# Attention stage of a decoder layer: three hardware loops written out, reciprocal sums moved to GpSimd, repeated score products dropped and four other products put into a gap of TensorE

## The reference, cut to what matters

```python
q = (x @ Wq + bq).reshape(1, B * N, H, hd)         # 2048 queries, 16 heads of 16
kv = (cond @ Wkv + bkv).reshape(1, -1, 2, H, hd)   # 2048 keys
q, k = _fq_sym(q * scale, axis=-1), _fq_sym(k, axis=-1)   # 8-bit grids
v = _fq_sym(v, axis=2)
attn = softmax(einsum('bhqd,bhkd->bhqk', q, k))
attn = _fq_unsigned(attn, axis=-1)                 # levels 0..255 of the row's largest weight
out = einsum('bhqk,bhkd->bhqd', attn, v) @ Wp + bp
```

## Time and profile before

| | |
|---|---|
| median of three runs | 2234.46 us (2227.49 to 2244.91) |
| the profiled execution, its own time | 2242.98 us |
| span of the profiled execution | 2241.2 us |
| mean granted TensorE clock over the span | 0.941 of full speed |
| busy share of the span | PE 82%, VectorE 75%, ScalarE 75%, GpSimd 24% |
| attention, first L1215 to last | 1206.3 to 2036.5 us, 830.2 us |
| attention in the 40 slices | about 22nd to 36th |

### The profile page before, as it was taken

One profiled execution on the slowest core, in us unless ns is written; L12 is line 12 of the kernel. 1 busy time (PEld: TensorE's weight loads), 2 busy tenths in 40 slices (PEclk: granted clock), 3 DMA queues, 4 the chain that ended last, 5 costly groups with the idle time before them and its releaser, 6 DMA issues. The chain is left out here.

```text
span 2241.2 us, 42040 instructions
## 1 busy us (share of the span) xinstructions
PE 1832.4 (82%) x12368; PEld 1273.1 (57%) x12514; DVE 1682.5 (75%) x2852; ACT 1673.6 (75%) x2987; POOL 527.5 (24%) x433
## 2 busy tenths in 40 slices
PE   6888999999999999999676667666676666664999
PEld 5776878777777777777453322222222222232887
DVE  5885676867777777777886888888878887886443
ACT  4667888888888888888368888888888887895211
POOL 2002555555555555555100000000000000002001
PEclk8998999999999999999899998899888998997999
DMA  4000000000000000000814998888888887896000
GB/s 133 15 5 29 0 28 0 28 0 28 0 28 0 28 0 28 0 28 0 174 26 83 167 166 156 154 164 164 160 152 160 161 163 150 161 166 145 10 10 19
DMA packets 566191, 173.18 MB, mean 77 GB/s; under 512 B 535168, under 2 KB 558592, under 8 KB 566144
## 3 DMA queue, kind: packets, MB, share of 16 engines
q1 hardware_dynamic: 566144, 172.57, 38.1%
HBM read 27.83 MB, written 2.10 MB: 13 GB/s over the span
## 5 line engine op out<-in xcount | busy, mean ns | idle before, releaser
L1278 ACT ACTIVATE levels<-s_ps,nb,qstep 128x512 int16<-128x512 f32 (+1 forms) x768 | 696.8, 915 | 118.8 <-DVE nb L1215 115.4
L1145 PE MATMUL s_ps<-kT,qT 128*128 128x512 bf16 x1451 | 492.0, 429 | 266.6 <-ACT levels L1278 253.4
L1204 DVE TENSOR_REDUCE mx<-s_ps 128x1 f32<-128x512 f32 (+1 forms) x768 | 636.6, 864 | 69.0 <-PE s_ps L1145 49.6
L603 DVE SCALAR_TENSOR_TENSOR xs<-x_ps,cw,xs 128x508 f32<-128x508 f32 (+2 forms) x393 | 291.1, 741 | 174.3 <-ACT xs L525 135.9
L1145 PEld LDWEIGHTS s_ps<-kT,qT 128*128 (+1 forms) x1532 | 117.7, 101 | 513.8 <-issue 488.5
L494 PE MATMUL o_ps<-wo,hid 128*128 x1024 | 242.9, 380 | 4.9 <-DVE acc L590 4.9
L659 POOL TENSOR_TENSOR hid<-y,sg 128x512 f32<-128x512 f32 x128 | 175.4, 1371 | 277.5 <-ACT sg L547 184.8
L1505 POOL MEMSET minus_half_o<- 128x4 f32 x1 | 0.1, 102 | 962.8 <-POOLq L1087 962.8
L494 PEld LDWEIGHTS o_ps<-wo,hid 128*128 128x128 f32 x1024 | 192.7, 189 | 39.5 <-issue 9.8
L1155 PEld LDWEIGHTS ao_ps<-vi,levels_T 128*128 128x128 f16 x4096 | 145.7, 98 | 82.7 <-issue 35.9
L525 ACT ACTIVATE xs<-x_ps,cb,cw 128x512 f32<-128x512 f32 x131 | 101.8, 777 | 116.5 <-PE x_ps L446 116.4
(11 more groups left out here) (200 smaller groups left out, 3220.5 us busy)
## 6 DMA issues: line engine op xcount, KB each, us to landing
w_raw<-winT_dram SPq DMA_DIRECT2D x18, 512.0 KB, 4.4
wo_raw<-woutT_dram SPq DMA_DIRECT2D x9, 512.0 KB, 5.7
kT<-zeros SPq DMA_DIRECT2D x4, 1024.0 KB, 19.4
qT<-zeros SPq DMA_DIRECT2D x4, 1024.0 KB, 16.0
levels_T<-levels SPq DMA_TRANSPOSE x256, 4.3
acc<-xT_dram SPq DMA_DIRECT2D x4, 512.0 KB, 6.1
w_bc<-winT_dram SPq DMA_DIRECT2D x16, 128.0 KB, 2.4
acc<-x_dram SPq DMA_DIRECT2D x1, 2048.0 KB, 11.5
```

The costliest lines, as they stand in the source:

```text
L603: dve.scalar_tensor_tensor(to, x_ps[:, :, 0:SEQ - s], cw[:, head, TAPS - 1 - s], to, ALU.mult, ALU.add).then_inc(chain if s < TAPS - 1 els ...
L1145: return pe.matmul(s_ps[:, BANKS[h % 2][chunk], :], qT[:, bass.ds(round_, 1), h % NH, :].rearrange("p b t -> p (b t)"), kT[:, h % NH, at:a ...
L1204: dve.tensor_reduce(mx[:, h % 2, at:at + 1], src, AX.XY if what == "cd" else AX.X, ALU.max).then_inc(max_done, 1)
L1278: act.activation(levels[:, s, at:at + banks * GT].rearrange("p (c k) -> p c k", c=banks), s_ps[:, bank:bank + banks, :], ACT.Exp, bias=nb[ ...
```

## The change: what it does

- The loops of all engines are written out over 256 units; `held` and the register waits go.
- `nstep` and `shift` are made once for all 16 rounds before the first unit, as three VectorE instructions on 128x256; `steps` goes.
- The partial sums are kept for two rounds only. GpSimd adds them and raises the total to the power -1 (three instructions on 128x16 for each round), after the last exponential of the round. `finish` on VectorE is left with the scaling, after a wait for GpSimd and for the value products. ScalarE waits for GpSimd before it overwrites the sums of two rounds ago.
- Chunk b is made once, not three times.
- `between` puts four matmuls of 256 columns each, of no use to the result, into the unused half of `ao_ps` at the start of each unit on TensorE, ahead of the wait for the exponential a. They are left out at unit 3 of rounds 1 to 15, while VectorE scales `ao_ps`.

```diff
-        nstep = sb("nstep", [P, NH])
-        shift = sb("shift", [P, NH])
+        nstep = sb("nstep", [P, BATCH, NH])
+        shift = sb("shift", [P, BATCH, NH])
-        sums = sb("sums", [P, BATCH, NH, 3])
+        sums = sb("sums", [P, 2, NH, 3])
...
         def _(pe):
...
-                    if exists(qt, h, 2):
-                        pe.wait_ge(b_exp, n + 1)
-                        pe.sem_inc(held, 1)
-                        for _ in range(2):
-                            score(qt, h + 2, "b")
-                        score(qt, h + 2, "b").then_inc(b_ready, 1)
...
+            def between():
+
+                for _ in range(4):
+                    pe.matmul(o_ps[:, E:2 * E], vi[:, 0, 0:P], vi[:, 1, :], start=True, stop=True)
...
+            for n in range(UNITS):
+                if n < NH or n % NH != LAG:
+                    between()
+                if n + 1 < UNITS:
+                    pe.wait_ge(a_exp, n + 1)
+                    score(n + 1, "a").then_inc(a_ready, 1)
+                if n + 2 < UNITS:
+                    pe.wait_ge(b_exp, n + 1)
+                    score(n + 2, "b").then_inc(b_ready, 1)
+                if n >= LAG:
+                    if n % NH == LAG and n >= NH:
+                        pe.wait_ge(scaled, n // NH)
+                    values(n - LAG)
+                if n + 2 < UNITS:
+                    pe.wait_ge(cd_exp, n + 1)
+                    score(n + 2, "c")
+                    score(n + 2, "d").then_inc(cd_ready, 1)
...
         def _(dve):
...
+            def finish(qt):
+
+                dve.wait_ge(tot_ready, qt + 1)
+                dve.wait_ge(pv_done, (qt + 1) * NH)
+                dve.tensor_tensor(att[:, qt, :].rearrange("p (h d) -> p h d", h=NH),
                                   o_ps[:, 0:E].rearrange("p (h d) -> p h d", h=NH),
+                                  rtot[:, qt % 2, :].unsqueeze(2).to_broadcast([P, NH, HD]), ALU.mult).then_inc(scaled, 1)
...
+            dve.tensor_scalar(nstep[:, :, :], qstep[:, :, :], -1.0, None, ALU.mult).then_inc(step_chain, 1)
+            dve.wait_ge(step_chain, 1)
+            dve.reciprocal(shift[:, :, :], nstep[:, :, :]).then_inc(step_chain, 1)
+            dve.wait_ge(step_chain, 2)
+            dve.tensor_scalar(shift[:, :, :], shift[:, :, :], LN255, None, ALU.mult).then_inc(step_chain, 1)
+            dve.wait_ge(step_chain, 3)
+            for n in range(UNITS):
+                maxima(n, "b")
+                if n % NH == LAG + 1 and n >= NH:
+                    finish(n // NH - 1)
+                maxima(n, "cd")
+                maxima(n, "a")
+                bias(n)
+            finish(BATCH - 1)
...
+            for n in range(UNITS):
+                act.wait_ge(nb_ready, n + 1)
+                if n % NH == 0 and n >= 2 * NH:
+                    act.wait_ge(tot_ready, n // NH - 1)
+                if n >= RING:
+                    act.wait_ge(turned[n % RING], n // RING * 16)
+                exps(n, "a", a_exp)
+                exps(n, "b", b_exp)
+                exps(n, "cd", cd_exp)
+
+        @block.gpsimd
+        def _(pool):
+            pool.memset(minus_one[:, :], -1.0).then_inc(chain, 1)
+            for qt in range(BATCH):
+                at = qt * 2 + 1
+                pool.wait_ge(cd_exp, (qt + 1) * NH)
+                if qt >= 2:
+                    pool.wait_ge(scaled, qt - 1)
+                pool.wait_ge(chain, at)
+                pool.tensor_tensor(part[:, :], sums[:, qt % 2, :, 0], sums[:, qt % 2, :, 1], ALU.add).then_inc(chain, 1)
+                pool.wait_ge(chain, at + 1)
+                pool.tensor_tensor(tot[:, :], part[:, :], sums[:, qt % 2, :, 2], ALU.add).then_inc(chain, 1)
+                pool.wait_ge(chain, at + 2)
+                pool.tensor_tensor(rtot[:, qt % 2, :], tot[:, :], minus_one[:, :], ALU.pow).then_inc(tot_ready, 1)
```

More of the change, by code:

```diff
@@ L1195, in _, with maxima @@
+            for n in range(UNITS - LAG, UNITS):
+                values(n)
         @block.vector
         def _(dve):
-            def maxima(n, h, what):
-                bank = BANKS[h % 2]
+            def maxima(n, what):
+                u = n % 2
+                bank = BANKS[u]
                 ready, at, src = {"b": (b_ready, 0, s_ps[:, bank["b"], :]),
@@ L1203, in maxima, with bias @@
                 dve.wait_ge(ready, n + 1)
-                dve.tensor_reduce(mx[:, h % 2, at:at + 1], src, AX.XY if what == "cd" else AX.X,
+                dve.tensor_reduce(mx[:, u, at:at + 1], src, AX.XY if what == "cd" else AX.X,
                                   ALU.max).then_inc(max_done, 1)
-            def bias(n, h):
-                u = h % 2
-                if not (isinstance(n, int) and n == 0):
+            def bias(n):
+                u = n % 2
+                qt, h = divmod(n, NH)
+                if n:
@@ L1249, in body @@
-            def body(qt):
-                for h in range(NH):
-                    n = qt * NH + h
-                    if exists(qt, h, 1):
-                        maxima(n + 1, h + 1, "b")
-                    if h == NH - 1 and exists(qt, h, 1):
-                        steps(qt + 1)
-                    if h == LAG and exists(qt, 0, -1):
-                        finish(qt, qt - 1)
-                    if exists(qt, h, 1):
-                        maxima(n + 1, h + 1, "cd")
-                        maxima(n + 1, h + 1, "a")
-                        bias(n + 1, h + 1)
@@ L1294, in _ @@
-            rounds(act, body)
+                               s_ps[:, bank:bank + banks, :], ACT.Exp, bias=nb[:, u:u + 1], scale=qstep[:, qt, h:h + 1],
+                               accum_out=sums[:, qt % 2, h, k:k + 1]).then_inc(done, 1)
+            for n in range(UNITS):
+                act.wait_ge(nb_ready, n + 1)
+                if n % NH == 0 and n >= 2 * NH:
+                    act.wait_ge(tot_ready, n // NH - 1)
+                if n >= RING:
+                    act.wait_ge(turned[n % RING], n // RING * 16)
+                exps(n, "a", a_exp)
+                exps(n, "b", b_exp)
+                exps(n, "cd", cd_exp)
```

148 lines of the change are left out of this document (33 added, 115 removed).

## The result

The changed kernel takes 2151.9 us (median of 4 runs, 2149.55 to 2154.47), the kernel before 2235.4 us in the same call (4 runs). The ratio is 0.9625, with a 95% interval of 0.9586 to 0.9665: 83.5 us are gone. The direction and the place were as forecast; the size was not.

What follows compares the result with a forecast made beforehand. Bound by a loop of latencies over two units in attention: 747.2 + 5.3 + 6.4 = 758.9 us instead of 830.2, +1.8 at the start, -0.7 at the end, so 2242.98 - 70.2 = 2172.8, said as 2173 us; range 2158 to 2210.

Steps and rivals of the forecast that it cites:

- What bounds the kernel: Attention stage: no engine is full; a loop of latencies over two units, with VectorE waiting 0.25 us for chunks c and d.
- Loops written out: Attention stage: a pair of units goes from 6.00 to 5.86 us, 747.2 us for 255 intervals between biases.
- a pair below 5.86: Attention stage: pairs shorter than forecast because c and d come earlier than thought; chance 0.04.
- Finish and the low stretches: Attention rounds: scaling left on VectorE costs 5.3 us, one stretch at half clock a round costs 6.4 us.
- The start: Before the first maximum: the block making the steps once for all rounds adds 1.8 us (0 to 3).
- The end: End of the attention stage: the three small operations of the last finish go, -0.7 us.
- The four products at full clock: TensorE's gap between chunks d and the next a: the products cost 0, covered by about 0.5 us.
- Rival 1: VectorE's bias waits for GpSimd's power, 1.0 us in each of 15 rounds, 15 us: 2188 us; chance 0.20.
- Rival 2: Attention rounds alternate between high and low clock: 2204 us in half of them (0.11), 2236 us in all (0.08).
- Rival 3: Transposing DMAs bound the attention stage, a pair takes 6.15 us: 2198 us; chance 0.08.
- Rival 4: TensorE's clock stays low in the attention stage and bounds it, 3.5 us a unit: 2309 us; chance 0.05.
- the turn with the steps: Turn of the hardware loop between rounds: its extra 1.12 us go 14 times, and that of round 0.

Runs made afterwards that it cites:

- a_undone: The changed kernel with everything put back except the hardware loop (increments, three copies of b without the four products, sums on VectorE, steps once a round): 2188.91 us.
- the fastest: The changed kernel with exponentials in the order a, cd, b, maxima cd, b, a, chunk b made three times and no four products: 2130.15 us.
- a_no_between: The changed kernel without the four products at the start of each unit, chunk b still made once: 2201.47 us.
- a_undone_between: The kernel of a_undone with chunk b made once and the four products instead of three copies of b: 2184.15 us.
- a_held: The changed kernel with the increments of semaphore held put back after the waits on both TensorE and VectorE: 2169.97 us.

## Why the prediction was right in direction and wrong in size

**What bounds the kernel.** Right: the loop of latencies over two units through c and d. It still shows its wait of 0.24 us once in a pair, and each increment put back into a link of it moves the pair and the stage. One reading was off without anything resting on it: the DMA share goes down to 0.79 in the slow round of rows 1, not only to 86%.

**Loops written out: "a pair goes from 6.00 to 5.87 us. I take 5.86."** This is the step that failed. I read the price of a written-out pair from round 0 of the kernel before. That round is free of the hardware loop, but not of the increments. They stand in all 16 rounds, since the written-out ones run the same body, and not only in the loop, as the words on the kernel before have it. The change takes them out as well, and I priced them nowhere. Each stood on the path, 0.06 us between the exponential and c, and 0.04 us for VectorE's ahead of the bias. Put back, they return the pair to 5.86 us. Without them it is 5.75: 127.5 x 5.75 = 733.1 us instead of 747.2, 14.1 of the 21.0 us by which the stage came out below the 758.9 us forecast. I had noted a pair below 5.86 as a case of 4 in 100, "because c and d come earlier than I think"; they do, and the reason was in the diff. For the loop alone 5.87 was right: that is the pair of a_undone.

**Finish and the low stretches: 5.3 + 6.4 us.** Mis-sized, 737.9 - 733.1 = 4.8 us together, 6.9 less than forecast. Finish costs 0.33 us (3.04 - 2.71) where it meets a full unit and nothing in the unit in which VectorE waits for c and d anyway: round 1 takes 45.96 us, just 8 x 5.75. The low stretches came, nine instead of sixteen, eight of them around unit 4 as forecast. One of them makes its round 46.21 us, 0.25 us longer, and exchanges the two kinds of unit, so that finish meets a full one in the next round (46.3 us). With three copies of b, where these stretches are missing, the whole stage is 0.8 us above its pairs (733.9 against 733.1); so finish by itself is nearly free, and some 4 of the 4.8 us come with the stretches. The three operations that left VectorE were 0.70 us, as taken, and putting them back costs 12.7 us, since the longer unit brings stretches at 1.2 GHz too.

**The start.** 1.8 us forecast; the timeline of VectorE shows the block as 2.44 us (1204.33 to 1206.77), where before it was 1.04, so +1.4:

```profile
1204.33 0.29 DVE L1206 TENSOR_SCALAR nstep<-qstep 128x256 f32<-128x256 f32 x1 [9.11 <-PEq L696]
1204.65 1.75 DVE L1208 RECIPROCAL shift<-nstep 128x256 f32<-128x256 f32 x1
1206.44 0.29 DVE L1210 TENSOR_SCALAR shift<-shift 128x256 f32<-128x256 f32 x1
1206.77 0.69 DVE L1184 TENSOR_REDUCE mx<-s_ps 128x1 f32<-128x512 f32 x1
```

**The end.** -0.7 forecast, +0.9 measured. The last scaling starts 9.20 us after the last bias, where in the kernel before, with the three small operations ahead of it, it was 9.03. So these 0.7 us did go, but the last product with the transposed levels starts 8.50 us after the last bias, where it was 7.70:

```profile
1955.63 0.60 PE L1136 MATMUL ao_ps<-vi,levels_T 128*128 128x16 f16 x16 [1.40 <-DMA levels_T<-levels]
1956.33 0.42 DVE L1202 TENSOR_TENSOR att<-ao_ps,rtot 128x256 f32<-128x256 f32 x1 [8.97 <-PE ao_ps L1136]
```

The rest lies in the output stage. Stage, first bias and end give -92.3 + 3.0 + 0.9 = -88.4 us, against 88.5 between the two profiled executions (2242.98 - 2154.47).

**The four products at full clock: 0.** Right: a's start above, and an undisturbed round takes 45.9 us with them and with three copies of b alike. That they and the single b are needed was not claimed, and the runs show that b's three copies would have done slightly better (by 5.6 us of the medians).

**Rival 1, the bias waits for the power.** Fell. The power is 2.91 us and done 3.6 us after the last exponential, where 2.90 and 3.7 were forecast, and a bias stands inside it (1443.49) with 0.22 us. That holds in each of the 15 rounds in which a bias starts inside the power, and no bias of the 256 takes longer:

```profile
L1194 DVE CUSTOM_DVE_ANT_0 low<-mx,shift,nstep x256: 221/222/223, 1209.2 to 1947.1; 128x3 f32<-128x3 f32 x128
```

By the Trainium skill (SBUF — State Buffer, section on the two separate sides) an operation with two SBUF inputs on VectorE that starts inside one of GpSimd's that reads SBUF would block until that one ends. Here the measurement decides: it did not for a power (0.22 us for the bias), as rows 12 had it; for the multiplication of rows 11 (1.35 us) it may hold.

**Rival 2, the clock alternates.** Not in this kernel. It does exist: with everything but the loop put back, two rounds run for the most part as pairs of 2.75 + 4.06 us, 53.3 us a round. The timeline of VectorE there:

```profile
1654.45 0.22 DVE L1202 CUSTOM_DVE_ANT_0 low<-mx,shift,nstep 128x3 f32<-128x3 f32 x1 [0.19 <-DVE mx L1190]
...
1657.20 0.22 DVE L1202 CUSTOM_DVE_ANT_0 low<-mx,shift,nstep 128x3 f32<-128x3 f32 x1 [0.19 <-DVE mx L1190]
...
1661.26 0.22 DVE L1202 CUSTOM_DVE_ANT_0 low<-mx,shift,nstep 128x3 f32<-128x3 f32 x1 [0.19 <-DVE mx L1190]
```

So what keeps it away is not the missing loop, and my argument against it, that it needed shifted work, does not hold by itself.

**Rival 3, the transposes bound.** Fell. The DMA share is 1.09 in rounds 1 and 2 of the changed kernel and 1.10 in the round shown of the fastest, which moves 188 GB/s with a pair of 5.58 us. The transposes land after 4.6 us in the median (4.3 before) and 6.6 at most, below the 7.4 us of cover. Least, median and most of the changed kernel:

```profile
DMA to landing us min/median/max: 4.3/4.6/6.6
```

**Rival 4, the clock stays low.** The clock stayed low in a_no_between, where nothing fills the gap, and that cost far less than I reckoned: not 66 us more than before, but 33 us less. I had taken 3.5 us for a unit at half clock; it is 3.08 (6.17 / 2). The rival had the four products in the way of chunk a, and a stage at half clock with them was not measured. Nor was my reason against it, that the clock rises again while TensorE works without a pause: in a_no_between it pauses (busy for 40.2 of 49.3 us at a clock of 0.50). The 4.06 us of an alternating unit are more than the clock: in a_undone_between, without the two copies of b in front of c and d, the long unit of such a pair is 3.65.

**Where the 83.5 us come from**, by the runs: 48.6 the loop (a_undone against before), 18.1 the increments, 12.7 the sums, 3.7 the steps, and -5.6 to +4.8 the four products, by what stands around them. These were taken one at a time and need not add up exactly: the parts other than the loop were 28.9 us singly and 37 together. Of the 71.3 us forecast for the stage, the plain pairs, the low stretches and the slow rounds had 42, the turn with the steps 18, finish 11, and the increments nothing.

## What to carry to other kernels

When the duration of a step is read from a stretch that "has the change already", compare its instructions with the diff line by line: round 0 had no loop but still had the increments, and these 0.11 us a pair were 14 of the 21 us by which the stage was off. In a loop of latencies, everything between a wait and the work it guards is on the path, a semaphore increment included, while a small operation on the waiting engine can be free in the unit that waits (the scaling in finish, 0.33 us) and costs its time in the one that does not. Filling a gap in TensorE's work is worth a lot where the clock would else stay low (49.6 us here), but price the filling that is already there before replacing it.

## What the runs showed of the hardware

- An increment of a semaphore behind a wait delays TensorE's next weight load by 0.06 us (medians of a_held and after, 0.11 against 0.05); on VectorE two of them delay the next instruction by 0.04 us (0.19 against 0.15).
- In a hardware loop, whose waits and addresses use registers, ScalarE's first exponential starts 0.38 us after the bias, and 0.27 us in the written-out rounds of the same kernel.
- At 1.2 GHz throughout, this stage, which is bound by latencies, loses 7% (pair 6.17 us in a_no_between against 5.75); where two extra chunks stand in front of the critical ones, a pair loses 0.95 us (a_undone, 2.75 + 4.06 against 2.75 + 3.11).
- GpSimd adds 128x16 in 0.21 to 0.23 us and raises 128x16 to a power in 2.91 us, and a VectorE bias (128x3) that starts inside the power is not delayed, in 15 cases of 15.
- After the first 10 us of the stage, two extra copies of 512 columns in every unit left no stretch at 1.2 GHz; four products of 256 columns left 7 to 12, in the three placements and with the two kinds of data that ran.
